# Context scan of a decoder layer: four consecutive times per partition, three row sums and one triangular product

## What is computed

```
    def _L0_xattn_ref(q, k, v):
        DECAY = 0.9
        kv = jnp.swapaxes(k * v, 0, 1)

        def step(r, kv_t):
            r = DECAY * r + kv_t
            return (r, r)
        ...
        return q * jnp.swapaxes(rs, 0, 1)
    ...
    x = _layernorm(x + _L0_attn_ref(x, ...), axis=-1)
    x = _layernorm(x + _L0_xattn_ref(x, ctx_1024, ctx_1024), axis=-1)
```

## Time and profile before

| | |
|---|---|
| median of 3 runs | 2942.02 us (2941.82 to 2942.49) |
| the profiled execution | 2942.34 us, span 2940.6 us |
| TensorE busy | 2698.1 us, 92% of the span |
| VectorE busy | 2122.7 us, 72% |
| ScalarE busy | 1264.8 us, 43% |
| GpSimd busy | 513.3 us, 17% |
| mean granted TensorE clock | 0.965 |
| steps 1 to 15 of the attention phase | 176 to 1211 us of the span, one every 69.46 us from step 2 on |

### The profile page before, as it was taken

The page is one execution under the profiler, slowest core; times in us unless marked ns, Lnnn a source line. Parts: engine busy times, 40 slices in busy tenths (PEclk is TensorE's granted clock), DMA queues, the critical chain, the costliest instruction groups (busy, mean ns, idle before and its releaser), DMA issues.

```text
span 2940.6 us, 33446 instructions
## 1 busy us (share of the span) xinstructions
PE 2698.1 (92%) x12016; PEld 2217.1 (75%) x12016; DVE 2122.7 (72%) x2561; ACT 1264.8 (43%) x1426; POOL 513.3 (17%) x305
## 2 busy tenths in 40 slices
PE   2489999999999999849999998899999969999998
PEld 2477777777777777638888887688888858888886
DVE  8668888888888888834444445587788776666664
ACT  2234333344343444333333332788888842222222
POOL 4211111111111111200000000122222223234332
PEclk7789999999999999979999999899999989999999
DMA  6311111211111111144545443677767673555453
GB/s 233 117 43 58 58 57 58 74 61 57 57 57 57 62 66 58 58 168 154 171 157 162 154 155 133 239 268 260 259 250 259 252 272 125 207 233 210 185 209 126
DMA packets 146957, 429.21 MB, mean 146 GB/s; under 512 B 74848, under 2 KB 83296, under 8 KB 106592
## 3 DMA queue, kind: packets, MB, share of 16 engines
q1 hardware_dynamic: 143312, 402.43, 37.7%
q10 hardware_dynamic: 3600, 26.22, 2.2%
HBM read 234.62 MB, written 177.21 MB: 140 GB/s over the span
## 4 chain that ended last, share of the span: by engine, by line
PE 52%; DVE 2%; DMA 1%; issue 1%; ACT 1%; POOL 0%; SPq 0%; POOLq 0%; DVEq 0%
PE ff_ps L1652 12%; PE ff_ps L1653 12%; PE ff_ps L1654 12%; PE ff_ps L1689 5%; PE ff_ps L1690 5%; PE ff_ps L1691 5%; DMA ff_w_stage<-w_ffn_t 1%; DVE ff_wl L1368 0%; DVE ff_sr L1574 0%; DMA ff_cand_g<-gate_ints 0%; DVE ff_lo L1374 0%; DVE ff_up_abs L1406 0%; DMA ff_q<-x_ints 0%; DMA gate_products<-ff_group 0%; ACT ff_wh L1202 0%
## 5 line engine op out<-in xcount | busy, mean ns | idle before, releaser
L1652 PE MATMUL ff_ps<-ff_hi,ff_wh 128*128 128x512 f32 x1536 | 600.0, 391 | 63.1 <-DVE ff_lo L1374 63.1
L1653 PE MATMUL ff_ps<-ff_lo,ff_wh 128*128 128x512 f32 x1536 | 599.5, 390 | 0.0
L1654 PE MATMUL ff_ps<-ff_hi,ff_wl 128*128 128x512 f32 x1536 | 599.4, 390 | 0.0
L1219 ACT ACTIVATE ff_group<-ff_ps,ff_scales 128x512 f32<-128x512 f32 x384 | 259.1, 687 | 333.7 <-PE ff_ps L1654 320.0
L1652 PEld LDWEIGHTS ff_ps<-ff_hi,ff_wh 128*128 128x128 f32 x1536 | 289.6, 189 | 124.2 <-DVE ff_lo L1374 63.9
L1654 PEld LDWEIGHTS ff_ps<-ff_hi,ff_wl 128*128 128x128 f32 x1536 | 289.5, 188 | 60.5
L1653 PEld LDWEIGHTS ff_ps<-ff_lo,ff_wh 128*128 128x128 f32 x1536 | 289.6, 189 | 60.3
L1689 PE MATMUL ff_ps<-ff_wh,ff_hi 128*128 128x512 f32 x768 | 300.1, 391 | 25.7 <-DVE ff_lo L1590 24.7
L1690 PE MATMUL ff_ps<-ff_wl,ff_hi 128*128 128x512 f32 x768 | 299.7, 390 | 0.0
L1691 PE MATMUL ff_ps<-ff_wh,ff_lo 128*128 128x512 f32 x768 | 299.7, 390 | 0.0
L1385 DVE TENSOR_REDUCE ff_gate_max<-ff_group 128x2048 f32 (+1 forms) x48 | 109.7, 2286 | 221.9 <-ACT ff_group L1219 221.9
(11 more groups left out here) (197 smaller groups left out, 5341.9 us busy)
## 6 DMA issues: line engine op xcount, KB each, us to landing
gate_products<-ff_group SPq DMA_DIRECT2D x48, 1024.0 KB, 4.0
ff_raw<-gate_products SPq DMA_DIRECT2D x48, 1024.0 KB, 5.6
up_products<-ff_group SPq DMA_DIRECT2D x48, 1024.0 KB, 4.2
ff_raw<-up_products SPq DMA_DIRECT2D x48, 1024.0 KB, 9.2
gate_ints<-ff_gs SPq DMA_DIRECT2D x48, 512.0 KB, 2.6
ff_gs<-gate_ints SPq DMA_DIRECT2D x48, 512.0 KB, 9.9
xt_raw<-in_xT SPq DMA_DIRECT2D x64, 256.0 KB, 2.8
csq<-in_ctx_rows SPq DMA_DIRECT2D x16, 1024.0 KB, 6.1
```

The lines of the kernel that those rows point to most:

```text
L1219: act.activation(group[:, g, m * T:(m + 1) * T], out_ps[(GM * g + m) % 6][:], ACT.Copy, scale=s_x).then_inc(evacuated, 1)
L1652: pe.matmul(o, wh[:, m, k], hi[:, par, k], start=(k == 0), stop=False)
L1653: pe.matmul(o, wh[:, m, k], lo[:, par, k], start=False, stop=False)
L1654: mm = pe.matmul(o, wl[:, m, k], hi[:, par, k], start=False, stop=(k == KC - 1))
```

## The change

Partition p now holds the four consecutive times 4p to 4p + 3 as its four rows (before: times p, 128 + p, 256 + p, 384 + p), for x, the context and the output. The square moves from GpSimd to ScalarE. VectorE makes three row sums within a partition (local_sums), each from the one before it. One triangular product, with decay 0.9^4 and a strip of 128 columns shifted by one partition, gives each partition the sum that arrives from those before it (context_carry, 3 matmuls); VectorE adds it to the four rows, times 0.9 to 0.9^4 (carried_sums). Only the last row is split into halves, the low half by VectorE (last_sum_low). The attention works on features by time, so that the projection must give rows in the new order: add_v writes the mixed value with time 4q + j at column 128 j + q, into a new buffer mixed_rows.

```diff
-        stripf = kv[:, 0]
+        stripf = kv[:, 0, 0:P]
...
-        scan_banks = [mix_ps[0][:], mix_ps[1][:], qk_ps[1][:, 0], qk_ps[1][:, 1]]
+        carry_bank = mix_ps[0][:]
...
                     if front:
-                        wait(sp, sql_ready, s)
+                        wait(sp, y_ready[1], TT * s)
                         sp.dma_start(csq[:], ctx_in[s]).then_inc(ctx_landed, 16)
...
                     if back:
-
-                        pool.wait_ge(ctx_landed, 16 * s)
-                        pool.tensor_tensor(csq[:], csq[:], csq[:], ALU.mult).then_inc(sq_ready, 1)
-                        pool.wait_ge(sqh_ready, s)
-                        pool.tensor_tensor(csq_l[:], csq[:], csq_h[:].bitcast(F32), ALU.subtract).then_inc(sql_ready, 1)
                         root(0, s)
                         root(1, s)
...
                         for m in range(KC):
                             act.wait_ge(mixed, KC * (s - 1) + m + 1)
-                            act.activation(ah[:, m], att[:, m], ACT.Copy).then_inc(mh_ready, 1)
+                            act.activation(ah[:, m], mixed_rows[:, m], ACT.Copy).then_inc(mh_ready, 1)
+                        act.wait_ge(ctx_landed, 16 * s)
+                        act.activation(csq[:], csq[:], ACT.Square).then_inc(sq_ready, 1)
                     if front:
                         front_tile(s, 1, par)
                     if back:
-                        act.wait_ge(sq_ready, s)
-                        wait(act, scan_ready, TT * (s - 1) if not isinstance(s, int) or s > 1 else 0)
-                        act.activation(csq_h[:], csq[:], ACT.Copy).then_inc(sqh_ready, 1)
+                        act.wait_ge(summed, (TT - 1) * s)
+                        wait(act, carry_ready, s - 1)
+                        act.activation(csq_h[:], csq[:, TT - 1], ACT.Copy).then_inc(sqh_ready, 1)
...
+                def local_sums(s):
+
+                    dve.wait_ge(sq_ready, s)
+                    for j in range(1, TT):
+                        dve.scalar_tensor_tensor(csq[:, j], csq[:, j - 1], XDECAY, csq[:, j],
+                                                 ALU.mult, ALU.add).then_inc(summed, 1)
+                        dve.wait_ge(summed, (TT - 1) * (s - 1) + j)
+
+                def last_sum_low(s):
+                    dve.wait_ge(sqh_ready, s)
+                    dve.tensor_tensor(csq_l[:], csq[:, TT - 1], csq_h[:].bitcast(F32), ALU.subtract).then_inc(sql_ready, 1)
+
+                def carried_sums(s):
+
+                    dve.wait_ge(carry_ready, s)
+                    for j in range(TT):
+                        dve.scalar_tensor_tensor(csq[:, j], carry_bank, XDECAY ** (j + 1), csq[:, j],
+                                                 ALU.mult, ALU.add).then_inc(scanned, 1)
+
...
-                        dve.wait_ge(scan_ready, n)
-
-                        dve.scalar_tensor_tensor(xrow[:, j], scan_banks[j], 1.0, xrow[:, j],
+                        dve.wait_ge(scanned, n)
+
+                        dve.scalar_tensor_tensor(xrow[:, j], csq[:, j], 1.0, xrow[:, j],
                                                  ALU.add, ALU.mult).then_inc(y_ready[1], 1)
...
-                    dve.scalar_tensor_tensor(att[:, m], att[:, m], 0.5, v_sb[:, 1 - par, m],
+                    dve.scalar_tensor_tensor(mixed_rows[:, m].rearrange("p (j q) -> p q j", q=P),
+                                             att[:, m].rearrange("p (q j) -> p q j", j=TT), 0.5,
+                                             v_sb[:, 1 - par, m].rearrange("p (q j) -> p q j", j=TT),
                                              ALU.mult, ALU.add).then_inc(mixed, 1)
...
                     if front:
                         front_product(s, 0)
-                        for c in range(1, KC):
-                            front_scans(s, c, par)
-                            front_product(s, c)
+                    if back:
+                        local_sums(s)
+                    if front:
+                        front_scans(s, 1, par)
+                        front_product(s, 1)
+                    if back:
+                        last_sum_low(s)
+                    if front:
+                        front_scans(s, 2, par)
+                        front_product(s, 2)
+                    if back:
+                        carried_sums(s)
+                    if front:
+                        front_scans(s, 3, par)
+                        front_product(s, 3)
...
-                        if j < 2:
-                            pe.wait_ge(gated, KC * (s - 1) + j + 3)
+                        if j == 0:
+                            pe.wait_ge(gated, KC * (s - 1) + 3)
+                        elif j == 1:
+                            pe.wait_ge(scanned, TT * s)
...
+                def context_carry(s):
                     pe.wait_ge(sql_ready, s)
...
+                    pe.wait_ge(gated, KC * s)
+                    product(carry_bank, [(strip_h[:], strip_l[:])], [(csq_h[:], csq_l[:])]).then_inc(carry_ready, 1)
...
                         for c in range(1, KC):
                             qkv(s, c)
+                            if back and c == 2:
+                                context_carry(s)
+                    elif back:
+                        context_carry(s)
...
                     if front:
                         broadcast(s)
-                    if back:
-                        context_scan(s, front)
```

More of the change, by code:

```diff
@@ L269, in attention_phase @@
         csq = sb("csq", [P, TT, HID])
-        csq_h = sb("csq_h", [P, TT, HID], F32R)
-        csq_l = sb("csq_l", [P, TT, HID], F32R)
+        csq_h = sb("csq_h", [P, HID], F32R)
+        csq_l = sb("csq_l", [P, HID], F32R)
+        mixed_rows = sb("mixed_rows", [P, KC, T])
         phi = sb("phi", [P, 2, 2, T])
@@ L339, in attention_phase @@
         norm_ready = [sem("norm1_ready"), sem("norm2_ready")]
-        sq_ready, sqh_ready, sql_ready, scan_ready = sem("sq_ready"), sem("sqh_ready"), sem("sql_ready"), sem("scan_ready")
+        sq_ready, sqh_ready, sql_ready, carry_ready = sem("sq_ready"), sem("sqh_ready"), sem("sql_ready"), sem("carry_ready")
+        summed, scanned = sem("summed"), sem("scanned")
         amax_step_ready, amax_taken = sem("amax_step_ready"), sem("amax_taken")
@@ L386, in _ @@
                 pool.memset(mhalf[:], -0.5).then_inc(const_pool, 1)
-                pool.memset(c09[:], XDECAY).then_inc(const_pool, 1)
+                pool.memset(c09[:], XDECAY ** TT).then_inc(const_pool, 1)
                 pool.memset(amax_x2[:], 0.0).then_inc(const_pool, 1)
@@ L784, in broadcast @@
                         pe.matmul(bc_banks[c], head_bc[:, c], rec_turned[:], start=True, stop=True).then_inc(bc_ready, 1)
-                def context_scan(s, front):
+                def context_carry(s):
                     pe.wait_ge(sql_ready, s)
-                    for j in range(TT):
-                        if j < 2:
-                            pe.wait_ge(y_ready[0], TT * s - j)
-                        elif front:
-                            pe.wait_ge(o_ready, KC * s + j - 1)
-                        stat = [(strip_h[:, (j - i) * P:(j - i + 1) * P], strip_l[:, (j - i) * P:(j - i + 1) * P])
-                                for i in range(j + 1)]
-                        mov = [(csq_h[:, i], csq_l[:, i]) for i in range(j + 1)]
-                        product(scan_banks[j], stat, mov).then_inc(scan_ready, 1)
+                    pe.wait_ge(gated, KC * s)
+                    product(carry_bank, [(strip_h[:], strip_l[:])], [(csq_h[:], csq_l[:])]).then_inc(carry_ready, 1)
                 def step(s, front, back):
@@ L1729 @@
         "xT": np.ascontiguousarray(a["x"].transpose(0, 2, 1)).reshape(NB, KC, P, T),
-        "x_rows": np.ascontiguousarray(a["x"].reshape(NB, TT, P, HID).transpose(0, 2, 1, 3)),
-        "ctx_rows": np.ascontiguousarray(a["ctx_1024"].reshape(NB, TT, P, HID).transpose(0, 2, 1, 3)),
+        "x_rows": np.ascontiguousarray(a["x"].reshape(NB, P, TT, HID)),
+        "ctx_rows": np.ascontiguousarray(a["ctx_1024"].reshape(NB, P, TT, HID)),
         "w_attn": np.ascontiguousarray(np.concatenate(
@@ L1751 @@
     rows = r.results[0]["out_rows"]
-    return np.ascontiguousarray(rows.transpose(0, 2, 1, 3)).reshape(NB, T, HID)
+    return np.ascontiguousarray(rows).reshape(NB, T, HID)
```

10 lines of the change are left out of this document (5 added, 5 removed).

## The result

The changed kernel takes 2949.75 us (median of 9 runs, 2948.75 to 2953.74), the kernel before beside it 2942.97 (9 runs). The ratio is 1.0026, 95% interval 1.0016 to 1.0036: 6.8 us slower. The interval leaves out no change at all, but not the 0.2% (5.9 us) up to which the prediction called it the same. The profiled execution has a span of 2948.6 us, against 2940.6. It has 432 TensorE matmuls fewer and TensorE is busy 71 us less, yet the kernel is not faster.

The account below looks back on a forecast made before the run. TensorE was taken as the bound, busy 67.43 of 69.46 us per attention period. The terms -1.5 + 19.7 - 37.0 + 10.2 + 11.9 + 4.7 gave +8.0 on 2942.0, so 2950.0 us, range 2932 to 2964.

Parts of the forecast that it names:

- Scan away, hole open: Attention loop, 14 step passages: 6.93 us scan goes, TensorE waits 6.19 for xl, then loses 2.15 at half clock; +19.7 us.
- Gate waits away: Gate, steps 2 to 15: GpSimd no longer holds up a VectorE scan, 2.64 us lost per step goes; -37.0 us.
- The carry: Before tile 3 and the projection: three matmuls, 0.68 us, in 15 steps; +10.2 us, slack 0.10 for the low half.
- The permuted write: VectorE's mixed-value write: x, its extra time over contiguous, 0.45 us, opens waits at gate and carry; 14 steps, +11.9 us.
- What is covered: Attention loop: VectorE's added work, ScalarE's square, carried sums and context load stay hidden; VectorE under 66 of 70 us.
- The ends: Start: narrower strip, -1.5 us; step 16: the carry stands before the last projection, +4.7 us.
- A: Rival, the 14 passages: TensorE keeps its full clock over the 6 us wait; 2919.5 us, chance 0.08.
- B: Rival, the permuted write: it costs nothing, x under 0.10, both slacks hold; 2937.7 us, chance 0.20.
- C: Rival, the permuted write: x about 0.75, waits of 1.45 us in 14 steps; 2958.7 us, chance 0.18.
- D: Rival, before tile 0: something lets tile 0 start at 725.3, so 117 us come off; 2833 us, chance 0.02.

Follow-up runs that it names:

- e5_cut: e3_square with only 4 of the context scan's 30 matmuls, so the context sum is mostly left out; 2924.05 us, ratio 0.9937.
- e1_fill: The changed kernel plus 27 unused matmuls on TensorE between the broadcast and tile 0 of the next batch; 2921.7 us, ratio 0.9931.
- e3_square: The kernel before with only the context's square moved from GpSimd to ScalarE; 2903.98 us, ratio 0.9869.
- e2_plain: The changed kernel with the mixed value written contiguously, not permuted, so output rows come in another order; 2939.28 us, ratio 0.9988.
- e6_high_first: The changed kernel with tile 0's 24 matmuls that read xh issued before the 12 that read xl; 2924.21 us, ratio 0.9937.
- e7_al_early: e6_high_first with the attention's high halves before ScalarE's norm and all low halves al before VectorE's second residuals; 2926.84 us, ratio 0.9945.
- e4_xl: The changed kernel with VectorE writing xl of parts 2 and 3 before the quotients; 2920.06 us, ratio 0.9923.
- e8_reorder: e7_al_early with L630 of gate tiles 0 and 1 between second residuals, sums and csq_l early, denominators beside project(2); 2989.52 us, ratio 1.0151.

## Why the prediction was right, point by point

The predicted 2950.0 and the forecast "slower, by a little" hold. Against the kernel before beside it (2942.97) the change costs 6.8 us, where 8.0 was predicted. Step by step, from the trace of after; the sum of the measured terms is +8.4, the spans differ by 8.0.

1. *Scan away, hole open* (+19.7 predicted, +23.7 measured). TensorE waits 6.2 us for xl, by broadcast to tile 0 6.29 more than before (7.42 against 1.13; 6.19 predicted). The slow stretch costs 2.33 us on average over the 14 passages, 1.46 to 3.01, where I took 2.15 from the mean of the earlier trace rows. -6.93 + 6.29 + 2.33 = +1.69, times 14. e5_cut shows this step alone (+20.1), e1_fill the clock alone. The term is 4 too small, within its bounds of 11.2 and 28.3.
2. *Gate waits away* (-37.0, measured -37). e3_square shows the cause, the square on GpSimd: with it alone gone the waits are 0.00 and 39 us come off.
3. *The carry* (+10.2): 0.68 us in each step, as predicted; 0.80 with the wait behind it, counted below.
4. *The permuted write* (+11.9 predicted, +8.3 measured). x was taken as 0.45; L635 takes 1094 ns against 685, x = 0.41. (The prediction says that every element lies 512 bytes from the one before; it is three such steps and one back, in groups of four.) The waits: gate 0.17 to 0.22 over the pitch (0.39 predicted), before the carry 0.25 or 0.33 and 0.12 in it (0.46). The step that was off is that the whole x lands on the path. L630 starts 0.91 and 0.93 us after the two L635 that precede it (750.19 to 751.10, 751.81 to 752.74), where a contiguous write gave 0.68 and 0.61: the duration grows by 0.41, the pitch by 0.23 to 0.32. In the kernel before and in the changed one:

```profile
749.61 0.66 DVE L617 SCALAR_TENSOR_TENSOR att<-att,v_sb 128x512 f32<-128x512 f32 x1
750.29 0.69 DVE L612 SCALAR_TENSOR_TENSOR att<-mix_ps,att 128x512 f32<-128x512 f32 x1
...
750.19 1.06 DVE L635 SCALAR_TENSOR_TENSOR mixed_rows<-att,v_sb 128x512 f32<-128x512 f32 x1
751.10 0.68 DVE L630 SCALAR_TENSOR_TENSOR att<-mix_ps,att 128x512 f32<-128x512 f32 x1
```

   In e2_plain these waits go, 0.52 of some 0.6 us a step; the 0.08 us that stay before the carry aren't the write's. The Trainium skill, "Vector Engine (DVE) Microarchitecture Reference", section "Measured stream behaviour on trn2", gave an estimate of x between 0.34 and 0.74; the trace's 0.41 lies near the lower end.
5. *What is covered*: it was. The square (1903 ns) delays nothing, phi 1 is not waited for, the context lands in time, and all scans take 1.22.
6. *The ends*: start -1.8 (122.60 against 124.39; -1.5 predicted), tail +5.0 (4.7): gate(16) starts at 1225.96 against 1222.64, the first feed-forward matmul at 1311.60 against 1303.27.

Two errors, the first term 4.0 too low and the fourth 3.6 too high, nearly cancel; that the sum came within half a microsecond is in part luck.

*The rivals.* A (the clock holds, 2919.5) falls: 0.50 behind each wait. Its price was nearly right, since e1_fill, in which the clock stays at 1.00, gives 2921.7. B (write free, 2937.7) and C (write dearer, 2958.7) fall by 1094 ns; B's price comes near e2_plain's 2939.3, but in part for another reason, since part of what e2_plain gains is a cheaper half clock. D (the hole isn't there, 2833) falls, and the runs say more than the prediction did: even a kernel without the hole would not give 2833. The 117 us that I gave for it leave out what VectorE delivers next, al and L630, at which e6_high_first (2924) and e7_al_early (2927) stop. The kernel with the hole and the wall gone is at 2871.

## What to carry to other kernels

Before counting matmuls that go, look at what TensorE would do in their place: if another engine's result is due only then, the matmuls were free, and taking them away cost, in this kernel, the clock's fall on top. Closing such a hole is worth only what lies between it and the next thing that the same slow engine delivers, so list all deliveries of that engine in one period, not the first one. And of a change in several parts, run each part alone: here one line of it was worth -39 us and the rest cost +46.

## What was not expected of the hardware

- TensorE's granted clock fell behind a wait of 2.46 us (e4_xl) too, while waits of 1.42 and 0.60 in the gate of before left it at 1.00. It falls late there: tile 0 begins at full clock and is at 0.50 from some 1.5 us on, as three stretches of e4_xl show:

```profile
714.27:715.50 1.23, 1.23 (x5) 1.04 (x6) 1.23 (x4) 0.08 (x1) 0.11 (x1) 1.00 0.00 0
715.50:717.00 1.50, 1.50 (x5) 1.16 (x4) 1.50 (x3) 1.50 (x3) 0.00 (x0) 0.59 0.00 0
717.00:718.00 1.00, 1.00 (x4) 0.80 (x3) 0.97 (x3) 1.00 (x2) 0.00 (x0) 0.50 0.00 0
```

- In the loop of the changed kernel the half clock costs 2.0 and 3.0 us in turn (1.99, 3.00, 2.02, 3.00), behind waits of the same 6.2 us. That is why the period alternates.
- In e8_reorder two waits of 2.38 and 3.02 us, 3 us apart, were followed by 17.6 us at 0.52. In the first 11.5 of them 512-column matmuls alternate with the 16-column ones of the denominators; then come almost only wide ones, at half clock as well. It was not settled whether the waits or the narrow matmuls made it so long.
- GpSimd's tensor_tensor over 128x2048 beside a VectorE scan: scan 4.57 us instead of 1.22. That is about the rest of the square when the scan starts (742.13 to 745.61, 3.48 us) and the scan's own 1.22. With GpSimd's square gone and its subtraction kept, the other scan keeps its mean of 2252 ns.
- ScalarE squares the same tile in 1903 ns. Neither in the changed kernel nor in e3_square does this stand beside a scan; it stands beside VectorE's subtractions of the low half al, which keep their time (four take 2.49 us; 683 ns each in e3_square). In the changed kernel:

```profile
757.24 2.49 DVE L666 TENSOR_TENSOR al<-mixed_rows,ah 128x512 fp32r<-128x512 f32 x4
757.98 1.90 ACT L473 ACTIVATE csq<-csq 128x2048 f32<-128x2048 f32 x1
```

- A VectorE write of 512 columns in groups of four, 512 bytes apart in a group: 1094 ns against 685, but the next instruction starts only 0.23 to 0.32 us later than behind the contiguous one.
